# Layer 0's routed experts: the inner width's last 48 rows stacked with their rounding rests, five down matmuls instead of six

## The reference, cut to what matters

```python
logits = x @ Wg.T                                   # 16 experts
topk_w, sel = jax.lax.top_k(softmax(logits), 4)     # four of them for each token
h = silu(einsum('td,efd->etf', x, W1)) * einsum('td,efd->etf', x, W3)   # f = 176
routed = einsum('etf,edf->td', h * combine.T[:, :, None], W2)           # d = 256
```

## Time and profile before

| what | value |
|---|---|
| median of 3 runs | 1327.85 us (1324.62 to 1328.19) |
| profiled execution, its own time | 1328.39 us |
| its span, first to last instruction | 1326.7 us |
| PE busy over the span | 987.1 us (74%) |
| DVE busy | 786.5 us (59%) |
| ACT busy | 601.8 us (45%) |
| POOL busy | 483.3 us (36%) |
| mean granted TensorE clock | 0.861 of 2.4 GHz |

### The profile page before, as it was taken

One profiled execution on the slowest core, in us unless ns is written; L12 is line 12 of the kernel. 1 busy time (PEld: TensorE's weight loads), 2 busy tenths in 40 slices (PEclk: granted clock), 3 DMA queues, 4 the chain that ended last, 5 costly groups with the idle time before them and its releaser, 6 DMA issues. The chain is left out here.

```text
span 1326.7 us, 21239 instructions
## 1 busy us (share of the span) xinstructions
PE 987.1 (74%) x5454; PEld 815.5 (61%) x5454; DVE 786.5 (59%) x1887; ACT 601.8 (45%) x1594; POOL 483.3 (36%) x646
## 2 busy tenths in 40 slices
PE   5356799999977688679999325558497960999990
PEld 2245678888866466569899213336385750788870
DVE  3764698999956753654444167788356652333333
ACT  0244798999953353555555112225232211333330
POOL 2345365666631773124444233334142421000005
PEclk9678799999987879799999757789698985999995
DMA  5235533333314232653333331100151003001004
GB/s 191 65 133 183 140 97 89 93 93 87 81 44 152 96 128 89 209 172 121 114 114 120 131 122 64 63 1 1 56 178 60 28 32 106 22 25 33 24 21 131
DMA packets 111890, 123.09 MB, mean 93 GB/s; under 512 B 46792, under 2 KB 85320, under 8 KB 111552
## 3 DMA queue, kind: packets, MB, share of 16 engines
q1 hardware_dynamic: 103408, 99.07, 25.3%
q0 software_dynamic: 8400, 23.01, 4.8%
HBM read 77.72 MB, written 44.32 MB: 92 GB/s over the span
## 5 line engine op out<-in xcount | busy, mean ns | idle before, releaser
L662 ACT ACTIVATE PR<-PS,nmax 128x128 f32<-128x128 f32 (+3 forms) x256 | 135.7, 552 | 9.8 <-DVE nmax L703 8.6
L580 POOL TENSOR_SCALAR PR<-PR,rinv 128x128 f32<-128x128 f32 (+3 forms) x256 | 131.6, 533 | 0.0
L703 DVE TENSOR_REDUCE nmax<-PS 128x1 f32<-128x128 f32 (+3 forms) x256 | 113.9, 483 | 24.0 <-PE PS L606 18.7
L1297 POOL DMA_INDIRECT r_results<-r_y,r_to x79 | 75.8, 959 | 135.9 <-DVE r_to L1348 84.1
L711 DVE TENSOR_TENSOR PTlo<-PS,PThi 128x512 fp32r<-128x512 f32 (+1 forms) x192 | 103.3, 593 | 2.9 <-ACT PThi L672 2.9
L672 ACT ACTIVATE PThi<-PS 128x512 fp32r<-128x512 f32 (+1 forms) x192 | 96.7, 545 | 11.5 <-PE PS L618 11.5
L605 PE MATMUL PS<-K,Q 128*128 128x128 f32 (+3 forms) x256 | 84.7, 391 | 10.5 <-PEq L259 5.7
L618 PE MATMUL PS<-ident,PR 128*128 128x128 f32 x640 | 87.9, 284 | 3.3 <-DVE PTlo L711 2.7
L2145 POOL DMA_INDIRECT x_yg<-x_results,d_slots x16 | 18.0, 1125 | 196.9 <-DMA x_results<-x_y 192.4
L634 PE MATMUL PS<-PThi,V 128*128 128x512 f32 (+3 forms) x256 | 85.1, 345 | 4.0 <-DMA V<-v_parts 3.0
L2198 DVE TENSOR_TENSOR x_h<-PS,x_sg 128x256 f32<-128x256 f32 x68 | 28.9, 425 | 92.9 <-ACT x_sg L2167 92.9
(11 more groups left out here) (356 smaller groups left out, 3123.3 us busy)
## 6 DMA issues: line engine op xcount, KB each, us to landing
r_xg<-r_sorted SPq DMA_DIRECT2D x79, 129.0 KB, 2.1
r_wst<-in_routed SPq DMA_DIRECT2D x16, 608.0 KB, 4.8
K<-k_parts SPq DMA_DIRECT2D x128, 64.0 KB, 1.8
c_yg<-r_results SPq DMA_DIRECT2D x16, 512.0 KB
v_parts<-vp SPq DMA_DIRECT2D x4, 1024.0 KB, 5.0
Q<-q_parts SPq DMA_DIRECT2D x64, 64.0 KB, 1.8
Q<-q_parts SPq DMA_DIRECT2D x128, 32.0 KB, 1.7
V<-v_parts SPq DMA_DIRECT2D x64, 64.0 KB, 2.1
```

The costliest lines, as they stand in the source:

```text
L580: pool.tensor_scalar(PR[:, e % 4, i, 0:w], PR[:, e % 4, i, 0:w], rinv[:, e % 4, i:i + 1], 1.0, ALU.mult, ALU.mult).then_inc(norm_done, 1)
L662: act.activation(PR[:, e % 4, i, 0:w], k.PS[:, i, 0:w], ACT.Exp, bias=nmax[:, e % 4, i:i + 1], accum_out=rsum[:, e % 4, i:i + 1]).then_inc ...
L703: dve.tensor_reduce(nmax[:, e % 4, i:i + 1], k.PS[:, i, 0:P * (i + 1)], AX_X, ALU.max, negate=True).then_inc(max_done, 1)
L1297: pool.indirect_dma_start(out=d.results, out_offset=bass.IndirectOffsetOnAxis(ap=to[:, i % TO_LANES:i % TO_LANES + 1], axis=0), in_=y[:, i ...
```

## The change

The second half of the transposed h had 48 rows in use and 80 empty ones, and yet took three matmuls. Now the same 48 values are written a second time, 64 columns further on, so that after the transpose they stand on partitions 0 to 47 and again on 64 to 111. ACT rounds the whole as before. DVE then overwrites the upper 64 partitions of `r_hhi`'s second half with the rests. One stationary tile so holds the rounded parts below and the rests above. The down weights' rows are doubled in the same way, in rows that were zeros before. A matmul of this tile with `whi` gives hi x hi and lo x hi at once; one with `wlo` gives hi x lo (and lo x lo, which is tiny). The first half still takes three matmuls, the second half two.

```diff
-        hhi, hlo = sb("hhi", [2, 2 * P], F32R), sb("hlo", [2, 2 * P], F32R)
+        hhi, hlo = sb("hhi", [2, 2 * P], F32R), sb("hlo", [2, P], F32R)
+        REST = L0_FF - P
@@ ACT, silu: the semaphore counts two for each block
-                wait(act, h_done, s - 1)
+                wait(act, h_done, 2 * (s - 1))
@@ DVE
             def times(s):
                 dve.wait_ge(sg_done, s + 1)
                 wait(dve, hT_ready, s - 1)
+                if s == 0:
+                    dve.wait_ge(zeroed, 2)
                 dve.tensor_tensor(h[:, s % 2, 0:L0_FF], PS_UP(s)[:, L0_FF:UP], sg[:, s % 2, :], ALU.mult).then_inc(h_done, 1)
+                dve.tensor_tensor(h[:, s % 2, P + HALF:P + HALF + REST], PS_UP(s)[:, L0_FF + P:UP], sg[:, s % 2, P:L0_FF],
+                                  ALU.mult).then_inc(h_done, 1)
             def split_h(s):
                 dve.wait_ge(hhi_done, s + 1)
-                dve.tensor_tensor(hlo[:, s % 2, :], PS_H(s), f32(hhi[:, s % 2, :]), ALU.subtract).then_inc(hlo_done, 1)
+                dve.tensor_tensor(hlo[:, s % 2, :], PS_H(s)[:, 0:P], f32(hhi[:, s % 2, 0:P]), ALU.subtract).then_inc(hlo_done, 1)
+                upper = hhi[HALF:P, s % 2, P:2 * P]
+                dve.tensor_tensor(upper, PS_H(s)[HALF:P, P:2 * P], f32(upper), ALU.subtract).then_inc(hlo_done, 1)
@@ PE (its waits on h_done and hlo_done are doubled too)
             def down(s):
-                pe.wait_ge(hlo_done, s + 1)
+                pe.wait_ge(hlo_done, 2 * (s + 1))
                 wait(pe, y_done, s - 1)
                 e = expert.pop(s)
-                for part in range(2):
-                    cols = slice(DM * UP + part * D, DM * UP + (part + 1) * D)
-                    f = slice(part * P, (part + 1) * P)
-                    last = split3_moving(pe, PS_Y(s), hhi[:, s % 2, f], hlo[:, s % 2, f],
-                                         moving(whi, e, cols), moving(wlo, e, cols), part == 0, part == 1)
-                last.then_inc(y_ready, 1)
+                first, rest = (slice(DM * UP + part * D, DM * UP + (part + 1) * D) for part in range(2))
+                split3_moving(pe, PS_Y(s), hhi[:, s % 2, 0:P], hlo[:, s % 2, :], moving(whi, e, first), moving(wlo, e, first), True, False)
+                pe.matmul(PS_Y(s), hhi[:, s % 2, P:2 * P], moving(wlo, e, rest), start=False, stop=False)
+                pe.matmul(PS_Y(s), hhi[:, s % 2, P:2 * P], moving(whi, e, rest), start=False, stop=True).then_inc(y_ready, 1)
@@ layout
     downs[:, :L0_FF] = a["L0_ffn_W2"].transpose(0, 2, 1)
+    downs[:, P + HALF:HALF + L0_FF] = downs[:, P:L0_FF]
```

More of the change, by code:

```diff
@@ L29 @@
 W_LANES = 3
+HALF = P // 2
 NOWHERE = 65536.0
@@ L1377, in up @@
                 pe.wait_ge(xlo_done, s + 1)
-                wait(pe, h_done, s - 1)
+                wait(pe, h_done, 2 * (s - 1))
                 for m in range(DM):
@@ L1387, in rows @@
                     pe.wait_ge(zeroed, 2)
-                pe.wait_ge(h_done, s + 1)
-                wait(pe, hlo_done, s - 1)
+                pe.wait_ge(h_done, 2 * (s + 1))
+                wait(pe, hlo_done, 2 * (s - 1))
                 pe.transpose(PS_H(s)[:, 0:P], h[:, s % 2, 0:P], k.ident[:])
```

## The result

The changed kernel takes 1331.75 us (median of 14 runs, 1328.98 to 1338.5), the kernel before 1327.89 us (14 runs, 1321.89 to 1332.15). The ratio is 1.0045, 95% interval 1.0026 to 1.0063: slower by 0.45%. It is taken from the means (1333.22 and 1327.29); the two medians alone would give 1.0029. The forecast was 1327.6 us and no change; the range 1322.5 to 1332.5 holds the time.

What follows compares the result with a forecast made beforehand. The hlo chain, 2.13 us per block, was taken as the floor, with late token loads interrupting. Steady part -0.4, weight stage +0.3 and last blocks -0.15 gave about -0.3 us: 1327.6 us, range 1322.5 to 1332.5.

Steps and rivals of the forecast that it cites:

- hlo chain: Steady part: loop from up product through ACT, DVE's r_hlo and PE's handing out to the next; 2.13 us per block.
- two limits on top of each other: Steady part: the matmuls need about as much, 2.115 us per block at most, as the hlo chain's 2.13.
- DVE's new instructions: Up to r_hlo's end: copy adds 0.12 us, split in two 0.07, together 0.19; bounds 0 to 0.35.
- held: DVE does not overlap across the partition change: r_hlo's second part ends another 0.08 us later, 1328.5 us; chance 0.22.
- The sequencer saves 0.04: PE's issuing of down: one weight load and one matmul fewer save 0.04 us, bounds 0 to 0.12.
- The floor's price: 64 steady blocks: 2.205 us per block in place of 2.13, summing to 141.1 us.
- A late load has more room: Steady part's late token loads: 0.325 us more room, leaving 4.1 us over 12 long periods, 0.5 for the others.
- r_y earlier: ACT: r_y starts about 0.10 us earlier behind the shorter down product, bounds 0 to 0.12.
- The weight stage and the tail: While weights arrive +0.3 us (0 to 0.6); last three blocks, without up product, -0.15 us.
- The clock: Array in the steady part: a rival had it idle more and fall to 1.2 GHz, a few us each; chance 0.03.
- The signs: Steady periods: right if shortest pairs 4.4 us and mean 2.26 to 2.30; wrong if pairs 4.0 to 4.1 or mean above 2.33.
- The hlo chain takes over: Slower rival, at down's handing out behind r_hlo's second part: delay 0.35 us instead of 0.19, 1331.2 us; chance 0.13.

Runs made afterwards that it cites:

- c: Changed kernel with VectorE's copy of the 48 columns moved behind the split of the hidden values: ratio 1.0024 to the kernel before.
- e: Changed kernel with PE waiting for the split's first half before the first three down matmuls, the second before the last two: ratio 0.9996 to the kernel before.
- a: Kernel before with its sixth down matmul left out, VectorE's instructions and the waits unchanged: ratio 0.9979 to the kernel before.
- b: Changed kernel with a sixth down matmul put back (its fourth issued twice), VectorE's new work kept: ratio 1.0056 to the kernel before.
- p: n with a sixth down matmul put back, repeating the fourth: ratio 0.9911 to the kernel before, 136.61 us for the 64 steady blocks.
- r: Kernel before, six down matmuls and no stacking, with VectorE's split in two 128-column halves and PE waiting for each separately: ratio 0.9996 to the kernel before.
- d: Changed kernel with the split's 64-partition subtraction replaced by one instruction over all 128 partitions: ratio 1.0010 to the kernel before.
- n: Changed kernel with copy behind the split, PE's split wait and 9 token buffers loaded 5 blocks ahead: 1320.43 us, ratio 0.9914 to the kernel before.
- m: Changed kernel with the edits of c and e together (copy behind the split, PE's split wait): ratio 0.9968 to the kernel before.
- h: Changed kernel with 9 token buffers instead of 8, each token load issued 5 blocks ahead instead of 4: ratio 0.9992 to the kernel before.

## Why the prediction was wrong, step by step

- **Which chain bounds: right.** The hlo chain was named, with its links, and "two limits on top of each other" too. Changing it alone moves the time (c, e), changing the array alone hardly (a, b, p).
- **"DVE's new instructions": the step that failed, by its size.** The prediction took 0.19 and measured is 0.31. Its parts: copy 0.12 as forecast (0.11 here, 0.115 by c). The split in two was put at 0.07, by overlap; it is 0.19. In r, where both parts have the same partitions, it is the 0.07. Of that 0.12 more, the hold makes nearly all: the second part starts 0.31 after the first instead of the 0.19 that d shows, and it runs 0.29, not 0.28. The bounds 0 to 0.35 held it. The rival "held" had the mechanism but counted the lost overlap of 0.08 only; the measured gap also has 0.03 between the end of one instruction and the start of the next. The Trainium skill states the hold in "VectorE: DVE Perf Modes", section "Two Vector instructions with no wait between them": an instruction whose operands start in another quadrant of partitions than those of the last one starts only after all earlier ones have finished. The trace agrees (0.31 against 0.19). It was the likelier detail by the prediction's own words and yet had 0.22 against 0.47. Standing on it as it was priced would have given 1328.5, still no change: its size was needed too.
- **"The sequencer saves 0.04": not seen.** 1.51 us from the split's end to the up product against 1.53, and b has the 1.51 with six matmuls too. With 0.31 and 0.02 the chain is 4.26 + 0.31 - 0.02 = 4.55, which is the pair. The prediction had 4.41; even so it named 0.25 as the point from which the slower rival decides.
- **The floor's price.** 0.29 a pair is 32 x 0.29 = +9.3 us, where the forecast had 64 x 0.075 = +4.8.
- **"A late load has more room": the direction fits, the size is open.** What lies above the floor was 146.12 - 136.6 = 9.5 and 147.60 - 137.3 = 10.3 us in before, and 2.7 and 8.5 in the changed kernel: 4.3 less on average. The forecast left 4.1 + 0.5 of 9.8, that is 5.2 less. The two profiles of the changed kernel lie 5.8 apart, so the average is worth little. With it, +9.3 - 4.3 = +5.0, against the ratios' +4.5 to +6.0 us (0.34 to 0.45% of 1328); that they agree so well is partly luck. Forecast for this stage was -0.4.
- **r_y earlier: right.** 645.59 to 646.45 is 0.86 against 0.96, the 0.10 forecast.
- **The weight stage and the tail.** +0.3 and -0.15 were too small to be seen in a spread of 3 us.
- **The clock: right.** 1.00 throughout the steady part.
- **The signs.** The shortest two periods in a row, 4.23, are the shortest with all stages running; the stretch of the earlier trace rows ends with a pair of 4.09, where no columns are left to do. The mean period is 2.32 in the first profile of the changed kernel and 2.41 in the second, above the 2.30 that was to show the forecast right; 2.33 was the sign of wrong.
- **The rivals.** "The hlo chain takes over" came true, with 0.31 where it was priced at 0.35. Its price, 1331.2, is 0.6 below the median, and it had only 0.13. I had valued the loads' relief rightly and the chain's growth by the hopeful half of its bounds.

## What to carry to other kernels

Where a matmul is cheap and overlapped, first ask whether its engine sets the pace; here 0.115 us a block off the array bought 0 to 0.4% in a and nothing that could be seen in p, and 0.31 us of small VectorE work ahead of the wait that hands out the next matmuls cost 0.4%. Count the instructions between a result and the wait for it, count an operation on other partitions as one that overlaps nothing before or behind it (0.31 instead of 0.20 us here), and let each consumer wait only for the part it reads. When two chains of nearly equal length lie on top of each other, look for a remedy for each: n, with both, took 1.2 to 1.3% off the changed kernel, where m and h alone had taken 0.7 to 0.8% and 0.4 to 0.5%.

## What the runs showed of the hardware

- VectorE's instructions with PSUM input follow each other by less than they last: 0.11 to 0.12 us after 48 columns (lasting 0.20), 0.20 after 128 (0.28), 0.25 after 176 (0.33), 0.34 after 256 (0.42). Each overlaps the next by some 0.08 to 0.09, as long as the partitions stay the same.
- Half the partitions save nothing: 64x128 takes 0.29 us, 128x128 0.28.
- The instruction behind the one on 64 partitions is held as well: r_to starts 0.33 after it (0.26 in d).
- A second wait in the midst of the down matmuls cost about 0.07 us a pair in e: its first part ends 0.02 earlier than before's whole split (0.98 against 1.00), and its pair is 0.05 longer. From the end of the part waited for first to the next up product it is 1.60 us in e (lower quartile) against 1.53 in before.
- One matmul with its weight load more or less in what is handed out in between changed that distance by 0.02 us at most: 1.51 in b and in the changed kernel, 1.52 in a and 1.53 in before.
